# First layer's experts: logits computed with experts on partitions behind each normalised group, and expert products ordered ahead of the gate

## The reference

```
xt = layernorm(x)                              # 2048 rows of 256
logits = xt @ router_w + router_b              # 2048 x 8
probs = softmax(logits)
gate = max(probs);  idx = argmax(probs)
y = gate * (xt @ expert_w[idx] + expert_b[idx])
x = x + y
```

## Time and profile before

| | |
|---|---|
| median of 3 runs | 6140.29 us (6135.06 to 6143.77) |
| profiled execution: its time, its span | 6141.55 us, 6139.7 us |
| granted TensorE clock, mean over the span | 0.930 |
| TensorE busy | 5456.5 us (89%) |
| VectorE busy | 3991.1 us (65%) |
| ScalarE busy | 2846.5 us (46%) |
| GpSimd busy | 1758.7 us (29%) |
| the stage of the change, from the first statistics to the next turns | 1562.76 to 1744.89 us |

### The profile page before, as it was taken

One profiled execution on the slowest core, in us unless ns is written; L12 is line 12 of the kernel. 1 busy time (PEld: TensorE's weight loads), 2 busy tenths in 40 slices (PEclk: granted clock), 3 DMA queues, 4 the chain that ended last, 5 costly groups with the idle time before them and its releaser, 6 DMA issues.

```text
span 6139.7 us, 76504 instructions
## 1 busy us (share of the span) xinstructions
PE 5456.5 (89%) x30068; PEld 2986.8 (49%) x30068; DVE 3991.1 (65%) x6950; ACT 2846.5 (46%) x4520; POOL 1758.7 (29%) x1903
## 2 busy tenths in 40 slices
PE   7987999999877879998998989998968879799978
PEld 4443454454544546555555653326834444333355
DVE  5666767767476669787987157763257755678632
ACT  4552444444105556656664236672135555366600
POOL 3201333333013117363655012202422122222021
PEclk8997999999789989998999889998979989899989
DMA  1000000000000000000000000004510000000033
GB/s 52 1 3 1 1 1 1 1 1 1 21 11 20 8 28 1 1 1 1 1 1 1 10 1 1 1 1 140 178 36 1 1 17 1 31 1 1 29 102 106
DMA packets 39365, 125.10 MB, mean 20 GB/s; under 512 B 5588, under 2 KB 20940, under 8 KB 32990
## 3 DMA queue, kind: packets, MB, share of 16 engines
q1 hardware_dynamic: 28206, 67.70, 3.2%
q0 software_dynamic: 10800, 52.52, 2.5%
HBM read 99.42 MB, written 24.90 MB: 20 GB/s over the span
## 4 chain that ended last, share of the span: by engine, by line


## 5 line engine op out<-in xcount | busy, mean ns | idle before, releaser
L74 PE MATMUL PS<-SC 128*128 128x128 f32 (+14 forms) x14896 | 2819.0, 428 | 168.5 <-ACT SC L80 60.1
L80 ACT ACTIVATE SC<-PS 128x1024 f32<-128x1024 f32 (+9 forms) x2553 | 1932.0, 782 | 1869.2 <-PE PS L74 1564.1
L74 PEld LDWEIGHTS PS<-SC 128*128 128x128 f32 (+6 forms) x14896 | 1217.1, 129 | 1507.9 <-issue 603.5
L95 DVE TENSOR_REDUCE SC<-PS 128x1 f32<-128x512 f32 (+5 forms) x2368 | 1514.7, 679 | 604.3 <-PE PS L74 592.5
L83 POOL TENSOR_TENSOR SC<-SC 128x1024 f32<-128x1024 f32 (+3 forms) x892 | 1189.1, 1343 | 1488.7 <-ACT SC L80 1247.4
L74 PE MATMUL PS<-AR 128*128 128x128 f32 (+6 forms) x4094 | 1148.9, 394 | 65.3 <-DVE SC L83 13.8
L74 PEld LDWEIGHTS PS<-AR 128*128 128x128 f32 (+2 forms) x4094 | 626.4, 179 | 467.2 <-issue 276.1
L77 PE MATMUL PS<-AR,SC 128*104 128x128 bf16 (+2 forms) x4660 | 524.9, 256 | 329.5 <-DVE SC L86 157.2
L74 PE MATMUL PS<-SC,AR 128*128 128x512 f32 (+7 forms) x1938 | 756.1, 513 | 46.1 <-POOL SC L83 12.7
L77 PEld LDWEIGHTS PS<-AR,SC 128*104 128x104 bf16 (+2 forms) x4660 | 406.3, 137 | 544.2 <-DVE SC L86 143.7
L80 ACT ACTIVATE SC<-SC 128x512 f32<-128x512 f32 (+7 forms) x870 | 445.1, 563 | 445.9 <-DVE SC L86 209.3
(11 more groups left out here) (82 smaller groups left out, 2164.1 us busy)
## 6 DMA issues: line engine op xcount, KB each, us to landing
SC<-in_pk11e SPq DMA_DIRECT2D x8, 1152.0 KB, 5.8
SC<-in_pk11e SPq DMA_DIRECT2D x8, 1028.0 KB, 5.0
xg<-SC SPq DMA_DIRECT2D x16, 512.0 KB, 7.0
SC<-yg SPq DMA_DIRECT2D x16, 512.0 KB, 8.0
yg<-AR SPq DMA_DIRECT2D x8, 512.0 KB, 6.1
AR<-in_pk SPq DMA_DIRECT2D x2, 1562.0 KB, 7.9
AR<-in_pk SPq DMA_DIRECT2D x2, 1538.0 KB, 13.0
AR<-in_pk SPq DMA_DIRECT2D x6, 512.0 KB, 4.9
```

What stands on the lines that cost most here:

```text
L74: return Step(self.real and self.real.matmul(*a, **k))
L80: return Step(self.real and self.real.activation(*a, **k))
L95: return Step(self.real and self.real.tensor_reduce(*a, **k))
```

## The change

`EarlyLogits` is the normalisation of this stage, now driven by `TopOne`. The router weights are copied into `wide`, two blocks of 32 columns of which the last 24 are zero. `wide` becomes the stationary operand and the turned rows stream past it, 512 at a time: the logits of group g land on partitions 32g to 32g + 31 of bank 0, with experts on partitions. TensorE issues them behind the turns of the following group. The router bias is spread over all partitions by one matmul of ones into `bb`. ScalarE copies all logits to `lt`, TensorE transposes them in four blocks, and VectorE adds `bb` and puts them in the old order. A small activation of `one` stands ahead of the softmax's exp on ScalarE.

The expert products follow the transposes of the logits at once. They use six banks (2 to 7) in place of eight, and product n waits for the sums of n - 6. The gate transposes of round k come behind the products of tile 4k + 1, and its bias products behind those of tile 4k + 2, in banks 0 and 1. VectorE adds the bias of round k ahead of the sums of tile 4k + 3. In ScalarE's order the square roots of the next normalisation stand between the copies of `GT`, and all copies of the next turned groups follow the last square root. The `Meet` between the normalisation and `TopOne` is gone.

```diff
--- before.py
+++ after.py
@@ -1286,7 +1286,38 @@
         e.wait_ge(vv, key(4))
+class EarlyLogits(Norm):
+    def __init__(self, K, tag, steps, stage):
+        self.stage = stage
+        super().__init__(K, tag, steps)
+    def pe(self, e):
+        pass
+    def act(self, e):
+        K, st = self.K, self.stage
+        for t in range(4 + self.lag):
+            self.tick_act(e, t)
+        self.act_turned(e, 0)
+        e.wait_ge(K.vv, "2 pad 0")
+        e.wait_ge(st.w.ready, "all")
+        e.activation(st.wide[:, :, 0:8], st.rw, ACT.Copy).then_inc(K.av, "2 pad")
+        for k in range(1, 4):
+            self.act_turned(e, k)
+    def dve(self, e):
+        e.memset(self.stage.wide, 0.0).then_inc(self.K.vv, "2 pad 0")
+        super().dve(e)
 class TopOne(Stage):
     next = None
@@ -1305,81 +1336,152 @@
         self.mx, self.sc, self.oh = take([NT]), take([NT, 8]), take([NT, 8])
         self.G = take([NT, 8])
         self.GT = take([2, 4, 128])
+        self.wide, self.lt, self.bb, self.one = take([2, 32]), take([512]), take([8]), take([1])
+        self.norm = EarlyLogits(K, "n2", [layer(K.X, take([NT, D]))], self)
+    def bank(self, n):
+        return 2 + n % 6
     def sums(self, e, g):
         e.wait_ge(self.K.vv, ("2 sum", 16 * g + 15, 1))
+        e.wait_ge(self.K.vv, ("2 bias", g, 1))
     def sp(self, e):
         e.dma_start(self.eb, self.K.ins["pk2e"]).then_inc(self.eb_ready, "all")
+    def pe_logits(self, e, g):
+        K = self.K
+        e.wait_ge(K.av, ("n2", "T", g, 1))
+        if g == 0:
+            e.wait_ge(K.av, "2 pad")
+        for c in range(2):
+            t = e.matmul(K.PS[32 * g:32 * g + 32, 0, :], self.wide[:, c, :], K.XNT[:, c, 512 * g:512 * g + 512], start=c == 0, stop=c == 1,
+                         tile_position=(0, 32 * g))
+        t.then_inc(K.mm, ("2 by expert", g))
+    def pe_gates(self, e, k):
+        K = self.K
+        e.wait_ge(K.vv, "2 gate")
+        if k == 0:
+            e.wait_ge(K.av, "2 lt")
+        else:
+            e.wait_ge(K.vv, ("2 bias", k - 1, 1))
+        for j in range(4):
+            t = e.transpose(K.PS[0:8, 0, 128 * j:128 * j + 128], self.G[:, 4 * k + j, :], K.ident)
+        t.then_inc(K.mm, ("2 GT", k))
+    def pe_bias(self, e, k):
+        K = self.K
+        e.wait_ge(K.av, ("2 GT", k))
+        if k == 0:
+            e.wait_ge(self.eb_ready, "all")
+            e.wait_ge(K.vv, "2 l")
+        else:
+            e.wait_ge(K.vv, ("2 bias", k - 1, 0))
+        for j in range(4):
+            t = e.matmul(K.PS[:, 1 - j // 2, 256 * (j % 2):256 * (j % 2) + 256], self.GT[0:8, k % 2, j, :], self.eb[0:8, :], start=True, stop=True)
+            if j % 2 == 1:
+                t.then_inc(K.mm, ("2 bias", k, j // 2))
     def pe(self, e):
         K, PS = self.K, self.K.PS
+        self.norm.pe_turn(e, 0)
+        for k in range(1, 4):
+            self.norm.pe_turn(e, k)
+            self.pe_logits(e, k - 1)
         e.wait_ge(self.w.ready, "all")
-        e.wait_ge(self.eb_ready, "all")
-        self.router.pe_logits(e, lambda c: self.rw[:, c, :], self.rb)
-        e.wait_ge(K.vv, "2 gate")
-        for k in range(4):
-            if k >= 2:
-                e.wait_ge(K.av, ("2 GT", k - 2))
-            for j in range(4):
-                t = e.transpose(PS[0:8, k % 2, 128 * j:128 * j + 128], self.G[:, 4 * k + j, :], K.ident)
-            t.then_inc(K.mm, ("2 GT", k))
-            e.wait_ge(K.av, ("2 GT", k))
-            for j in range(4):
-                if k >= 2 and j % 2 == 0:
-                    e.wait_ge(K.vv, ("2 bias", k - 2, j // 2))
-                t = e.matmul(PS[:, 2 + 2 * (k % 2) + j // 2, 256 * (j % 2):256 * (j % 2) + 256], self.GT[0:8, k % 2, j, :], self.eb[0:8, :],
-                             start=True, stop=True)
-                if j % 2 == 1:
-                    t.then_inc(K.mm, ("2 bias", k, j // 2))
-        e.wait_ge(K.vv, ("2 bias", 3, 1))
+        e.matmul(PS[:, 2, 0:8], K.ones[0:1, 0:128], self.rb, start=True, stop=True).then_inc(K.mm, "2 bb")
+        self.pe_logits(e, 3)
+        e.wait_ge(K.av, "2 lt")
+        for j in range(4):
+            t = e.transpose(PS[:, 1, 128 * j:128 * j + 128], self.lt[:, 128 * j:128 * j + 128], K.ident)
+        t.then_inc(K.mm, "2 logits")
         for i in range(NT):
             for e2 in range(4):
                 n = 4 * i + e2
-                if n >= 8:
-                    e.wait_ge(K.vv, ("2 sum", n - 8, 1))
+                if n >= 6:
+                    e.wait_ge(K.vv, ("2 sum", n - 6, 1))
+                elif n == 0:
+                    e.wait_ge(K.av, "2 bb")
                 for c in range(2):
-                    t = e.matmul(PS[:, n % 8, :], K.XNT[:, c, 128 * i:128 * i + 128],
+                    t = e.matmul(PS[:, self.bank(n), :], K.XNT[:, c, 128 * i:128 * i + 128],
                                  self.ew[:, c, 2 * e2:2 * e2 + 2, :].rearrange("p e n -> p (e n)"), start=c == 0, stop=c == 1)
                 t.then_inc(K.mm, ("2 experts", n))
+            if i % 4 == 1:
+                self.pe_gates(e, i // 4)
+            if i % 4 == 2:
+                self.pe_bias(e, i // 4)
         if self.next is not None:
             for k in range(4):
-                e.wait_ge(K.vv, ("2 sum", 4 * NT - 8 + 2 * k + 1, 1))
+                if k == 0:
+                    e.wait_ge(K.vv, ("2 bias", 3, 1))
+                else:
+                    last = max(n for n in range(4 * NT) if self.bank(n) == 2 * k + 1)
+                    e.wait_ge(K.vv, ("2 sum", last, 1))
+                    last = max(n for n in range(4 * NT) if self.bank(n) == 2 * k)
+                    e.wait_ge(K.vv, ("2 sum", last, 1))
                 self.next.pe_turn(e, k)
     def act(self, e):
         K = self.K
+        e.wait_ge(K.mm, "2 bb")
+        e.activation(self.bb, K.PS[:, 2, 0:8], ACT.Copy).then_inc(K.av, "2 bb")
+        for g in range(4):
+            e.wait_ge(K.mm, ("2 by expert", g))
+        e.activation(self.lt, K.PS[:, 0, :], ACT.Copy).then_inc(K.av, "2 lt")
+        e.activation(self.one, K.ones[:, 0:1], ACT.Exp).then_inc(K.av, "2 table")
         self.router.act_softmax(e)
         for k in range(4):
             e.wait_ge(K.mm, ("2 GT", k))
             if k >= 2:
                 e.wait_ge(K.mm, ("2 bias", k - 2, 1))
-            e.activation(self.GT[0:8, k % 2], K.PS[0:8, k % 2, :].rearrange("p (j n) -> p j n", j=4), ACT.Copy).then_inc(K.av, ("2 GT", k))
+            e.activation(self.GT[0:8, k % 2], K.PS[0:8, 0, :].rearrange("p (j n) -> p j n", j=4), ACT.Copy).then_inc(K.av, ("2 GT", k))
+            if self.next is not None:
+                self.next.tick_act(e, k)
         if self.next is not None:
-            self.next.act_all(e)
+            for k in range(4):
+                self.next.act_turned(e, k)
+    def dve_bias(self, e, k):
+        K = self.K
+        for j2 in range(2):
+            v = K.X[:, 4 * k + 2 * j2:4 * k + 2 * j2 + 2, :]
+            e.wait_ge(K.mm, ("2 bias", k, j2))
+            e.tensor_tensor(v, v, K.PS[:, 1 - j2, :].rearrange("p (j n) -> p j n", j=2), ALU.add).then_inc(K.vv, ("2 bias", k, j2))
     def dve(self, e):
         K, X, G, PS = self.K, self.K.X, self.G, self.K.PS
-        self.router.dve_logits(e)
+        e.wait_ge(K.mm, "2 logits")
+        e.wait_ge(K.av, "2 bb")
+        e.tensor_tensor(self.router.l.rearrange("p (g j) e -> p g j e", g=4), PS[:, 1, :].rearrange("p (j g e) -> p g j e", j=4, g=4)[:, :, :, 0:8],
+                        bc(self.bb.unsqueeze(1).unsqueeze(1), [128, 4, 4, 8]), ALU.add).then_inc(K.vv, "2 l")
+        e.wait_ge(K.vv, "2 l")
         self.router.dve_softmax(e)
         p = self.router.p
         self.router.dve_first_max(e, p, self.mx, self.sc, self.oh, "top")
         e.tensor_tensor(G, self.oh, p, ALU.mult).then_inc(K.vv, "2 gate")
         e.wait_ge(K.vv, "2 gate")
-        for k in range(4):
-            for j2 in range(2):
-                v = X[:, 4 * k + 2 * j2:4 * k + 2 * j2 + 2, :]
-                e.wait_ge(K.mm, ("2 bias", k, j2))
-                e.tensor_tensor(v, v, PS[:, 2 + 2 * (k % 2) + j2, :].rearrange("p (j n) -> p j n", j=2), ALU.add).then_inc(K.vv, ("2 bias", k, j2))
-        e.wait_ge(K.vv, ("2 bias", 3, 1))
         for i in range(NT):
+            if i % 4 == 3:
+                e.wait_ge(K.vv, ("2 sum", 4 * i - 1, 1))
+                self.dve_bias(e, i // 4)
+                e.wait_ge(K.vv, ("2 bias", i // 4, 1))
             for e2 in range(4):
                 n = 4 * i + e2
                 e.wait_ge(K.mm, ("2 experts", n))
                 for k in range(2):
                     if e2 > 0 or k > 0:
                         e.wait_ge(K.vv, ("2 sum", n, 0) if k else ("2 sum", n - 1, 1))
-                    e.scalar_tensor_tensor(out=X[:, i, :], in0=PS[:, n % 8, 256 * k:256 * k + 256], scalar=G[:, i, 2 * e2 + k:2 * e2 + k + 1],
```

(4 more changed lines are left out.)

## The result

The changed kernel takes 6100.7 us at the median of four runs (6100.5 to 6104.2), the kernel before 6139.2 (6135.1 to 6143.8). The ratio is 0.9943, with an interval of 0.9931 to 0.9955: 35.0 us less, 27.6 to 42.4. The forecast was 6113.5 with a range of 6101 to 6123; the medians lie 38.5 us apart, where I had put 26.8 on the likeliest case and 37.0 on the first rival, the rise of the clock inside the logits. The direction was right. The likeliest case was not what happened; its rival was. 6100.7 itself lies just under the 6101 at which the range ended; the kernel before had 6140.3 when that range was worked out and has 6139.2 here, and 38.5 or 35.0 less than 6140.3 is 6101.8 or 6105.3.

A forecast was written before the change was run, and what follows sets the result against it. TensorE alone, at 1.2 GHz, was taken to set the time of the old logits. Experts starting 36.0 us earlier, less 9.2 for the bias inside, save 26.8 us: 6113.5 us, range 6101 to 6123 for 8 in 10.

The forecast's parts named there:

- the likeliest case: New logits stay at 1.2 GHz and bias rounds keep the clock: 26.8 us saved, 6113, own range 6108 to 6119; 62%.
- the first rival: Clock rises to 2.4 GHz inside the new logits: 10.2 us more, 37.0 saved, 6103.3 us; 15%.
- The step that failed: New logits, 32 columns of weights with full transposes between them, were held at 1.2 GHz to the end.
- the 64-column products: Evidence against a rise in the logits: dense products from 2790.12 on, still at 1.2 GHz between 2794 and 2796.
- The first logits: Start on TensorE at 1575.1, after the clearing of `wide`, ScalarE's first two copies and the small copy into `wide`.
- The tile's price: Extra cost of 32-column tiles in the logits: 0.3 us per group, 1.2 in all.
- A round: Gate transposes and bias products inside the expert stream at 2.4 GHz: 2.3 us per round, 9.2 in all.
- The gate and the banks: VectorE's gate takes 4.2 us beside the expert products; six banks let TensorE run ahead, with 7.5 us of cover.
- not to become the bound: In the expert stream VectorE spends 1.00 us per product of 1.71 and lags some 5 us, below six products (10.3).
- The tail: Four ScalarE copies of the next normalisation move behind its last square root; cost 0 to 0.5 us, taken as 0.
- The second rival: Bias rounds in the expert stream lose the clock; four falls cost 10.6 to 13.2 us; 14% for some of this.
- The slower case: Bias rounds inside the expert stream hold TensorE at 1.2 GHz: 45 us added, 6158; 2%.

The follow-up runs named there:

- e5: The changed kernel, but each group's logits are the old 128x8 products with the bias as a third matmul; stage 162.0 us, 6118.1 us.
- e10: The changed kernel with the logits of group 0 issued four times over, sixteen 32-column passes in a row; stage 151.1 us, 6102.4 us.
- e6: The changed kernel with 128 columns of weights in the logits and no column tiles; stage 145.5 us, 6101.2 us.
- e8: The changed kernel with each round's bias products issued four times over, 32 passes instead of 8; stage 183.3 us, 6130.1 us.
- e9: The changed kernel with three banks for the expert products in place of six; stage 147.6 us, 6101.3 us.
- e4: The changed kernel with all logits behind all turns, so no transposes stand between them; stage 140.5 us, 6101.4 us.
- e11: The changed kernel with all logits behind all turns, 128 columns of weights and no column tiles; stage 145.2 us, 6094.1 us.
- v3: e4 with the bias row ahead of all logits and ScalarE's copies of groups 0 and 1 between its square roots; 6085.2 us against 6130.5, ratio 0.9925.
- e3: The changed kernel without the small exp ahead of the softmax's; stage 145.75 us, 6097.5 us.
- e1: The kernel before with only the new logits; gate, bias rounds and experts in the old order with eight banks; 6116.5 us against 6137.7, ratio 0.9965.
- v4: v3 with nine products of constants in TensorE's pauses around the first turns; stage 138.7 us, 6089.4 us, ratio 0.9931.

## Why the prediction was right and where it was wrong

**The step that failed** is the one that carried the likeliest case: "so I hold them at 1.2 GHz to the end". The forecast had the experts start 33.5 us into the stage and their first 5.3 us low; they started at 25.6, all of them at 2.4 GHz. The first rival had said 26.0 and 37.0 us saved, and the stage saved 36.4. I had the mechanism, its time and its price, and gave it 15%. That the time lies at the edge of the range for 8 in 10 is owed to this rival, which the range took in; the likeliest case, with its own 6108 to 6119, missed.

What I weighed wrongly was the evidence against it. The stretch of 128x8 products says something about products that stream eight columns. e5 shows that these don't bring the clock in the new place either, and e10 that 512 columns past a 32-column operand bring it in 5.4 us with nothing else between. So the old logits were no witness for the new ones. The other, the 64-column products, I read in one window only, and took as evidence of a clock that stays low. The window over their start says something else:

```profile
2790.00:2792.00 2.00, 1.88 (x4) 0.47 (x4) 0.15 (x1) 0.66 (x2) 0.00 (x0) 0.83 0.00 0
```

They began at 1.00, behind a wait of 2.75 us, and the clock fell at 2791.3, 1.2 us into them. They end at 2796.17, after 4.8 us at the low clock. Where the clock rose in these kernels, it did so between 3.3 and 6.4 us after the dense work began, so 4.8 us at 0.50 say little. In the same trace sixteen passes of that shape ran from 2477.17 to 2484.18 at 1.00 throughout. A full width of 128 columns isn't needed, by e10, and with it the clock rises at nearly the same place, by e6.

The Trainium skill ("TensorE: Matmul & The Clock Gate", Part 1) would have given the right answer for the new logits by its rule that sustained activity releases the throttle: the trace agrees in the kernel after and in e10. It would have given the wrong one for the old, where e5 stays at 0.50 with TensorE busy throughout, and for e8, where 8-row passes lose the clock. I took the failure on the old logits as one on the whole, and that was the mistake.

**The rest of the sum, term by term.** The first logits start 12.25 us into the stage, predicted 12.3. The tile's price was put at 1.2 us in four groups and is about 0.3 by e6. A round was to cost 2.3 us and costs 0.44 + 1.92 = 2.36 by its own starts; the expert stream is 120.1 us long where the rival's terms give 112.6 - 2.65 + 9.2 = 119.2, so the four rounds cost 10.2 instead of 9.2, about 2.5 each, the rest being in the products beside them. The rival's missing 0.6 us is this 0.9, less 0.3 by which the experts start earlier than its terms gave.

**The gate and the banks.** 4.2 us were predicted for the gate and 4.2 measured; no wait for sums appeared, as forecast, and e9 shows that half the banks would nearly have done.

**VectorE** was not to become the bound. Its group of scalings in the kernel after, against the earlier trace rows:

```profile
L89 DVE SCALAR_TENSOR_TENSOR AR<-PS,SC,AR 128x256 f32<-128x256 f32 x128 | 61.7, 484 | 39.9 <-PE PS L74 36.3
```

It is still idle for 39.9 us among them. **The tail** was taken as 0 with a bound of 0.5; ScalarE's last copy in the kernel after, against the earlier trace rows:

```profile
1713.19 0.60 ACT L80 ACTIVATE AR<-PS 128x512 f32<-128x512 f32 x1 [0.26 <-PE PS L77]
```

It starts 7.9 us after the first turn, before 7.7: 0.2 lost.

**The second rival** didn't happen in the kernel after, and e8 shows how it could have: there the fall comes 4.5 to 5.5 us into such passes, and a round of the kernel after is over in 1.9. **The slower case** fell with the same observation.

**What stays open.** The runs don't separate what it is in the 128x8 and the 8-row passes that fails to bring or hold the clock. The time spent loading weights alone isn't it: it is 1.93 of 2.00 us in e5's window, 1.61 in e8's and 0.35 to 0.55 in e10's, but 2.00 of 2.00 in the window of e4 just ahead of the rise. Why the rise came 3.6 us after the dense transposes began in e4, 5.5 and 6.4 after the same ones in e11 and v3, and anywhere from 3.3 us (the last round of e8) on elsewhere, isn't settled: I didn't vary what stands ahead of it. Why ScalarE's table load sat at the end of a wait before the change and ahead of it in e3 isn't either. And the start of the stage, which moves by 10 us between kernels with the same code ahead of it, wasn't looked into.

## What to carry to other kernels

A matmul that streams a few columns past a large stationary operand costs twice: TensorE loaded weights for 1.93 of 2.00 us in e5's window, and dense as they were, such passes left the clock at 1.2 GHz, for 23.7 us in the kernel before and longer in e5. Turning the product round, so that hundreds of columns stream past the narrow operand, cut the logits and brought the clock for what follows. In the kernel after a wait of 0.69 us behind them did no harm; in e1 one of 4.34 us lost the clock. When a stretch of the trace is used as a witness about the clock, compare the whole shape of its products with the new ones, streamed columns and stationary ones, and read the windows on both sides until the clock changes.

## What the runs showed of the hardware

**Column tiles run at once.** Three groups on three tiles took 1.93 us (e4), four took 2.40 (v4), one alone 1.90, and the same three without tiles 6.17 (e11, the first 1.7 at 1.2 GHz). The Trainium skill ("TensorEngine Tiling (Array Packing)", Key Properties) says that different tiles can load and multiply in parallel; these runs agree, and the kernel after shows a condition: with full transposes between the groups, the second and third take 1.83 us each. The price of the changes of mode, which I had put at 0.3 us a group, comes to about 0.1 a group over the four of e6, unevenly: 0.27 for the second group and its turn, 0.01 for the third group.

**A fully busy TensorE can lose its clock.** In e8 it fell from 2.4 to 1.2 GHz 4.5 to 5.5 us into 8-row passes without any idle time, in each of four rounds, and came back 3.3 to 5.8 us after dense 128-row products resumed.

**It can rise inside dense transposes.** In e4 it rose 3.6 us into sixteen full transposes, with nothing but turns on TensorE in the 15 us before. It doesn't always: in e11 and v3 the same transposes ended first, after about 4 us, and it rose in the logits behind them. Products of constants in the pauses held it at 1.00 through the turns (v4).
